# Token attention fused with the first expert dispatch, and a re-split dispatch: one TensorE, ScalarE and VectorE program in place of two

## What is computed

```python
# token attention, per image; xn is the token's row norm (mean 0, variance 1 over 128 channels)
scores = xn @ xn.T
x = x + softmax(scores) @ xn
# mixture of experts: per token
xn = (x - mean(x)) * rsqrt(var(x) + eps)
scores = xn @ Wg + bg                       # 8 experts
topk_vals, topk_idx = top_k(scores, 2)
gates = softmax(topk_vals)
out = sum over the 2 chosen experts: gate * (gelu(xn @ W1[e] + b1[e]) @ W2[e] + b2[e])
```

## Time and profile before

| | us |
|---|---|
| median of 3 runs | 2566.55 (2564.8 to 2569.15) |
| profiled execution | 2577.6 |
| its span in the trace | 2575.5 |

### The profile page before, as it was taken

One profiled execution on the slowest core, in us unless ns is written; L12 is line 12 of the kernel. 1 busy time (PEld: TensorE's weight loads), 2 busy tenths in 40 slices (PEclk: granted clock), 3 DMA queues, 4 the chain that ended last, 5 costly groups with the idle time before them and its releaser, 6 DMA issues. The chain is left out here.

```text
span 2575.5 us, 54220 instructions
## 1 busy us (share of the span) xinstructions
PE 1827.2 (71%) x16654; PEld 1267.9 (49%) x16654; DVE 1792.5 (70%) x5249; ACT 1274.2 (49%) x2662; POOL 1443.4 (56%) x1552
## 2 busy tenths in 40 slices
PE   7999998998943222777745788888432209999993
PEld 4555556775742221555533355555322207777772
DVE  5888886775767662666642899998476627888873
ACT  5777764655620001555530678776210007777760
POOL 4555560000137773777765466666477745676675
PEclk9999998998965555999975899998555559999995
DMA  5000000000022113656637000000441136777757
GB/s 115 3 0 0 0 1 1 0 1 1 0 81 92 54 54 107 176 169 177 182 113 180 1 1 0 0 0 2 115 160 54 54 112 217 231 230 230 232 172 299
DMA packets 191639, 232.97 MB, mean 90 GB/s; under 512 B 60384, under 2 KB 157397, under 8 KB 184046
## 3 DMA queue, kind: packets, MB, share of 16 engines
q1 hardware_dynamic: 164302, 172.32, 23.0%
q0 software_dynamic: 26880, 52.27, 6.0%
q10 hardware_dynamic: 288, 6.42, 0.6%
HBM read 155.37 MB, written 79.23 MB: 91 GB/s over the span
## 5 line engine op out<-in xcount | busy, mean ns | idle before, releaser
L2311 POOL DMA_INDIRECT expert_out<-moe_yr,moe_to x448 | 494.8, 1104 | 268.9 <-DVE moe_yr L2290 148.0
L2082 POOL DMA_INDIRECT expert_rows<-d_row,d_pos x392 | 380.2, 970 | 167.8 <-issue 118.0
L2226 ACT ACTIVATE moe_ah<-moe_hps,moe_w 128x512 f32<-128x512 f32 (+1 forms) x336 | 230.3, 686 | 204.4 <-PE moe_hps L2176 202.2
L2267 DVE TENSOR_TENSOR moe_hl<-moe_ah,moe_hh 128x512 fp32r<-128x512 f32 (+1 forms) x336 | 236.3, 703 | 98.0 <-ACT moe_hh L2231 92.2
L1851 PE MATMUL d_rank<-d_seen,d_below 128*128 128x32 bf16 (+1 forms) x50 | 10.4, 207 | 346.7 <-DVE d_seen L1983 346.7
L1851 PEld LDWEIGHTS d_rank<-d_seen,d_below 128*128 128x128 bf16 x50 | 5.2, 104 | 351.3 <-DVE d_seen L1983 351.3
L549 POOL TENSOR_TENSOR window_pr<-window_pr,window_rc 113x392 f32<-113x392 f32 x128 | 108.9, 851 | 107.1 <-DVE window_rc L493 107.0
L2174 PE MATMUL moe_hps<-moe_xh,moe_w 128*128 128x512 f32 (+1 forms) x336 | 138.5, 412 | 35.1 <-DMA moe_w<-moe_split 25.6
L2162 PE MATMUL moe_xps<-ident,moe_xb 128*128 128x128 f32 x448 | 73.5, 289 | 119.4 <-DMA moe_xb<-expert_rows 119.4
L1939 DVE TENSOR_SCALAR d_row<-d_xt,d_mv,d_rs 128x128 f32<-128x128 f32 x196 | 67.1, 404 | 111.9 <-DMA expert_rows<-d_row,d_pos 111.8
L2186 PE MATMUL moe_yps<-moe_hh,moe_w 128*128 128x512 f32 (+1 forms) x336 | 143.7, 428 | 0.9 <-DVE moe_hl L2267 0.9
(11 more groups left out here) (262 smaller groups left out, 5482.1 us busy)
## 6 DMA issues: line engine op xcount, KB each, us to landing
moe_w<-moe_split SPq DMA_DIRECT2D x56, 1026.5 KB
moe_xb<-expert_rows SPq DMA_DIRECT2D x112, 264.0 KB
moe_w<-moe_split SPq DMA_DIRECT2D x56, 449.5 KB
final_yy<-expert_out SPq DMA_DIRECT2D x28, 448.0 KB
c_yy<-expert_out SPq DMA_DIRECT2D x48, 256.0 KB
expert_out<-moe_yr,moe_to POOLq DMA_INDIRECT x448, 3.4
X<-in_x SPq DMA_DIRECT2D x32, 196.0 KB
expert_rows<-d_row,d_pos POOLq DMA_INDIRECT x392
```

The source lines that it names most:

```text
L2082: pool.indirect_dma_start(out=rows_dram, out_offset=bass.IndirectOffsetOnAxis(ap=pos[j][:, i, k:k + 1], axis=0), in_=row[j][:, i, :], in_o ...
L2226: act.activation(ah[n % NH][0:P, :], hps[n % 3][0:P, :], func, bias=bias(b, k)[0:P]).then_inc(h_done, 1)
L2267: dve.tensor_tensor(hl[n % NH][0:P, :], ah[n % NH][0:P, :], hh[n % NH][0:P, :].bitcast(F32), ALU.subtract).then_inc(hl_done, 1)
L2311: pool.indirect_dma_start(out=y_dram, out_offset=bass.IndirectOffsetOnAxis(ap=to[j][:, t:t + 1], axis=0), in_=yr[j][:, t, :], in_offset=No ...
```

## The change

Two stages become one, and the dispatch is written anew as a class that both places use.

- `token_dispatch_phase` replaces the token stage and "d2". One step of the token pipeline handles a group (392 tokens) and, where enough tokens have their residual, a chunk of the dispatch (512 tokens). `sorting_steps` gives the step at which a chunk is transposed: with residuals done up to group s-2 at step s, chunks fall at steps 3, 4, 5, 7, 8, 9, 11, and so on to 34, three chunks in four steps with one extra. A chunk is transposed in step s, gets logits and is chosen in s+1, and is weighed and placed in s+2.
- PSUM is shared out anew: one bank for the centred tokens (two before), one bank `tps` for both the turned probabilities and the turned tokens, two for transposed tiles, and one bank `small` for logits and ranks together. So `logits(c)` waits for `at_done` of chunk c-1, an instruction of `place`.
- GpSimd does nothing but scatters. The product of the probabilities (L1078 before) is on VectorE (`probs`), and the copy of the turned tokens out of PSUM (L1014 before) is on ScalarE (`v_out`).
- The row norm of the dispatch is on ScalarE as four Identity activations for a chunk with `scale` the reciprocal deviation and `bias` the negated product of mean and reciprocal deviation, which VectorE makes (`negmean`). Two column copies of VectorE also go to ScalarE (`names`); two more instructions of `weigh` and the addition of the region's base in `place` are gone (the base is in the ranks' product, which is why REGION is now a multiple of 1024). The second gate weight has its sign turned, and the expert stage adds where it subtracted.
- SyncE writes the pads once the table is there, without waiting for the scatters.
- "d3" uses the same class, with four banks of transposed tiles, one step for each chunk.

The core of the diff (the bodies of `choose`, `stats`, `table`, `positions` and of the token attention's functions are those of before but for names, buffers and what is said above):

```diff
@@ module level @@
-REGION = TOKENS + BLOCK
+REGION = 13 * 1024
+CHUNKS = chunk_tiles()
...
+class Dispatch:
+    NR = 3
...
+    def pads(self, sp):
+        sp.wait_ge(self.loaded, 16 * 8)
+        spare = self.rows_dram[EXPERTS * REGION:EXPERTS * REGION + BLOCK].rearrange("(t p) c -> p t c", p=C)
+        sp.dma_start(spare, self.pad[:, :, :]).then_inc(self.padded, 16)
+        sp.wait_ge(self.tab, 2)
+        for x in range(EXPERTS):
+            n = sp.value_load(self.offs[0:1, x:x + 1], min_val=0, max_val=EXPERTS * REGION - BLOCK)
+            sp.dma_start(self.rows_dram[bass.ds(n, BLOCK)].rearrange("(t p) c -> p t c", p=C), self.pad[:, :, :]).then_inc(self.padded, 16)
+        for j in range(2):
+            sp.wait_ge(self.w_stored[j], 32 * EXPERTS // 2)
+        sp.wait_ge(self.b_stored, 16)
+        sp.wait_ge(self.padded, 16 * (EXPERTS + 1))
...
+    def logits(self, pe, c):
+        t0, nt = CHUNKS[c]
+        if c >= 1:
+            pe.wait_ge(self.at_done, c)
+        for i in range(nt):
+            last = pe.matmul(self.small[:, i * EXPERTS:(i + 1) * EXPERTS], self.sh.X[:, (t0 + i) * C:(t0 + i + 1) * C], self.wgc[:, :],
+                             start=True, stop=True, skip_group_check=True)
+        last.then_inc(self.log_mm, 1)
...
+    def norm(self, act, q):
+        c, t0, nt, o = QUADS[q]
+        j = c % self.NR
+        act.wait_ge(self.nm_done, q + 1)
+        act.wait_ge(self.rs_done, q + 1)
+        if c >= self.NR:
+            act.wait_ge(self.scattered[j], 16 * self.scatters(c - self.NR))
+        for i in range(nt):
+            last = act.activation(self.row[j][:, o + i, 0:C], self.xt[q % len(self.xt)][:, i * C:(i + 1) * C], ACT.Identity,
+                                  bias=self.nm[q % 2][:, i:i + 1], scale=self.rs[c % 2][:, o + i:o + i + 1])
+        last.then_inc(self.normed, 1)
+    def gate(self, act, c):
+        nt = CHUNKS[c][1]
+        act.wait_ge(self.gap_done, c + 1)
+        if c >= 1:
+            act.wait_ge(self.den_done, c)
+            act.wait_ge(self.col_done, c)
+        act.activation(self.ex[:, 0:nt], self.gap[:, 0:nt], ACT.Exp).then_inc(self.ex_done, 1)
+    def names(self, act, c):
+        t0, nt = CHUNKS[c]
+        j = c % self.NR
+        act.wait_ge(self.loaded, 16 * 8)
+        if c >= self.NR:
+            act.wait_ge(self.scattered[j], 16 * self.scatters(c - self.NR))
+        act.activation(self.row[j][:, 0:nt, C], self.tokens[:, t0:t0 + nt], ACT.Copy).then_inc(self.named, 1)
+        act.wait_ge(self.idf_done, c + 1)
+        act.activation(self.row[j][:, 0:nt, C + 1], self.idf[:, 0:nt, 0], ACT.Copy).then_inc(self.named, 1)
...
+    def prepare(self, dve):
+        dve.memset(self.count[0][:, :], 0.0).then_inc(self.count_done, 1)
+        dve.memset(self.base16[:, :], 0.0).then_inc(self.ready, 1)
+        dve.wait_ge(self.loaded, 16 * 8)
+        dve.wait_ge(self.ready, 1)
+        dve.tensor_copy(self.base16[0:1, :], self.base8[0:1, :]).then_inc(self.ready, 1)
+        dve.tensor_copy(self.below[:, :], self.below_f[:, :]).then_inc(self.ready, 1)
+        dve.tensor_copy(self.ones[:, :], self.ones_f[:, :]).then_inc(self.ready, 1)
+        dve.wait_ge(self.centred, 1)
+        dve.tensor_copy(self.wgc[:, :], self.small[:, 0:EXPERTS]).then_inc(self.ready, 1)
...
+    def negmean(self, dve, q):
+        c, t0, nt, o = QUADS[q]
+        dve.wait_ge(self.rs_done, q + 1)
+        if q >= 2:
+            dve.wait_ge(self.normed, q - 1)
+        dve.scalar_tensor_tensor(out=self.nm[q % 2][:, 0:nt], in0=self.mv[q % 2][:, 0:nt, 0], scalar=-1.0, in1=self.rs[c % 2][:, o:o + nt],
+                                 op0=ALU.mult, op1=ALU.mult).then_inc(self.nm_done, 1)
...
+    def weigh(self, dve, c):
+        nt, j = CHUNKS[c][1], c % self.NR
+        row = self.row[j]
+        dve.wait_ge(self.ex_done, c + 1)
+        if c >= 1:
+            dve.wait_ge(self.g0_done, c)
+        dve.tensor_scalar(self.den[:, 0:nt], self.ex[:, 0:nt], 1.0, None, ALU.add).then_inc(self.den_done, 1)
+        dve.wait_ge(self.den_done, c + 1)
+        if c >= self.NR:
+            dve.wait_ge(self.scattered[j], 16 * self.scatters(c - self.NR))
+        dve.reciprocal(row[:, 0:nt, C + 2], self.den[:, 0:nt]).then_inc(self.g0_done, 1)
+        dve.wait_ge(self.g0_done, c + 1)
+        dve.scalar_tensor_tensor(out=row[:, 0:nt, C + 3], in0=self.ex[:, 0:nt], scalar=-1.0, in1=row[:, 0:nt, C + 2],
+                                 op0=ALU.add, op1=ALU.mult).then_inc(self.col_done, 1)
+    def place(self, dve, c):
+        nt, j, h = CHUNKS[c][1], c % self.NR, c % 2
+        dve.wait_ge(self.pos_mm, c + 1)
+        if c >= 1:
+            dve.wait_ge(self.spot_done, c)
+        dve.tensor_tensor(self.at[:, 0:nt, :, :], self.pick[h][:, 0:nt, :, :],
+                          self.ranks(nt).rearrange("p (t e) -> p t e", e=EXPERTS)[:, :, None, :].to_broadcast([C, nt, 2, EXPERTS]),
+                          ALU.mult).then_inc(self.at_done, 1)
+        dve.wait_ge(self.at_done, c + 1)
+        if c >= 1:
+            dve.wait_ge(self.pos_done, c)
+        dve.tensor_reduce(self.spot[:, 0:nt, :], self.at[:, 0:nt, :, :], AX_X, ALU.add).then_inc(self.spot_done, 1)
+        dve.wait_ge(self.spot_done, c + 1)
+        dve.tensor_copy(self.pos[j][:, 0:nt, :], self.spot[:, 0:nt, :]).then_inc(self.pos_done, 1)
...
+    def scatter(self, pool, c):
+        nt, j = CHUNKS[c][1], c % self.NR
+        pool.wait_ge(self.pos_done, c + 1)
+        pool.wait_ge(self.normed, LAST_QUAD[c] + 1)
+        pool.wait_ge(self.col_done, c + 1)
+        pool.wait_ge(self.named, 2 * c + 2)
+        for i in range(nt):
+            for k in range(2):
+                pool.indirect_dma_start(out=self.rows_dram, out_offset=bass.IndirectOffsetOnAxis(ap=self.pos[j][:, i, k:k + 1], axis=0),
+                                        in_=self.row[j][:, i, :], in_offset=None).then_inc(self.scattered[j], 16)
...
+def sorting_steps(groups_done):
+    turns, step = [], 0
+    for c, t0, nt, o in QUADS:
+        while groups_done(step) * T < (t0 + nt) * C:
+            step += 1
+        turns.append(step)
+        step += 1
+    return turns
+def token_dispatch_phase(nc, sh, kind, e, wsplit, rows_dram):
...
+    LEAD = 4
...
+        cps, st, tps, sps, ops_ = ps("cen", [C, 512]), ps("st", [C, 512]), ps("turn", [C, 512]), ps("sps", [C, 512]), ps("ops", [C, 512])
+        d = Dispatch(nc, sh, sb, sem, kind, e, wsplit, rows_dram, [ps(f"xt{i}", [C, 512]) for i in range(2)], ps("small", [C, 512]))
...
+            for s in range(-LEAD, last_step):
+                if group(s + 1):
+                    scores(s + 1)
+                if group(s + 3):
+                    var(s + 3)
+                if group(s - 1):
+                    values(s - 1)
+                if group(s):
+                    turn(s)
+                if group(s + 2):
+                    tokens(s + 2)
+                for c in chunks(s - 2):
+                    d.positions(pe, c)
+                for c in chunks(s - 1):
+                    d.logits(pe, c)
+                for q in quads(s):
+                    c, t0, nt, o = QUADS[q]
+                    pe.wait_ge(res_done, -(-(t0 + nt) * C // T))
+                    d.turn(pe, q)
+                if group(s + 4):
+                    mean(s + 4)
+            d.totals(pe)
...
+            for s in range(-LEAD, last_step):
+                if group(s + 1):
+                    shift(s + 1)
+                if group(s - 1):
+                    residual(s - 1)
+                for q in quads(s - 1):
+                    d.negmean(dve, q)
+                if group(s + 1):
+                    probs(s + 1)
+                if group(s + 3):
+                    norm(s + 3)
+                for c in chunks(s - 2):
+                    d.weigh(dve, c)
+                    d.place(dve, c)
+                for c in chunks(s - 1):
+                    d.choose(dve, c)
+                for q in quads(s):
+                    d.stats(dve, q)
+                if 1 <= s <= EXPERTS:
+                    d.split_low(dve, s - 1)
+            dve.wait_ge(res_done, NG)
+            d.table(dve)
...
+            for s in range(-LEAD, last_step):
+                if group(s + 1):
+                    expo(s + 1)
+                for q in quads(s - 1):
+                    d.rstd(act, q)
+                if group(s + 3):
+                    rstd(s + 3)
+                if group(s):
+                    turned(s)
+                if group(s + 2):
+                    v_out(s + 2)
+                for q in quads(s - 1):
+                    d.norm(act, q)
+                for c in chunks(s - 2):
+                    d.gate(act, c)
+                    d.names(act, c)
+                if 1 <= s <= EXPERTS:
+                    d.split_high(act, s - 1)
+                if group(s + 4):
+                    square(s + 4)
...
@@ dispatch_phase, the expert stage and build @@
+        turns = sorting_steps(lambda step: NG)
...
```

(37 more changed lines are left out.)

## The result

The changed kernel takes 2521.9 us in the median of four runs (2519.8 to 2524.2), the kernel before beside it 2567.9 (2564.8 to 2572.7): ratio 0.982, 95% interval 0.980 to 0.984. The forecast was 2515, in a range of 2470 to 2560: the sign, the size and the mechanism came out. Within the sum the end of each dispatch was about 7 us short, and in the fused stage the term for the clock, about 9 us too large, covered that.

A forecast was written before the change was run, and what follows sets the result against it. VectorE's queue, through waits on ScalarE and TensorE, was taken to bound the fused stage, GpSimd's scatters the second dispatch. Fused stage -47, clock +12, second dispatch -16.5 make -51.5: 2515 us on the median's scale, range 2470 to 2560.

The forecast's parts named there:

- the term for the clock: Fused stage: TensorE's low clock adds 1.4 us a step, 41 us in 29 steps, of which 30% was taken, +12.
- VectorE's queue bounds the fused stage: Fused stage: VectorE's queue, through waits on ScalarE and TensorE, takes 13.3 us a chunk against GpSimd's 10.1.
- The forecast's layout of a full step: Fused stage, step with place, choice and stats, timed from VectorE's shift: `gate` ends at 6.25, the step takes 12.3 us.
- The row norm on ScalarE: Fused stage: four 128-column activations ahead of `gate`, between 0.8 and 2.4 us, taken as 1.1.
- its sum at the high clock: Attention and first dispatch fused, steps laid out at the high clock: 380 us against 427, -47.
- The pads: End of second dispatch: 13.0 us from first pad to next stage become a barrier's 1.7, -11.3.
- the earlier start: Second dispatch: the first chunk is placed sooner, ahead of the second split of the weights, about -5 us.
- Low clock throughout: Rival: TensorE stays at the low clock in the fused stage, total 2546 us; chance 0.20.
- GpSimd as the bound: Rival: GpSimd's scatters remain the bound, fused stage 315 us, total 2438; chance 0.09.
- Slower by a mean step of 12.2 us: Rival: single banks at the low clock delay the residual, 12.6 us a step, total 2579, deciding from 12.2; chance 0.09.
- the sign that the prediction named for this rival: Fused stage: VectorE waits for the residual's product in most steps, 2.1 us late in every step.
- Second dispatch unchanged: Rival: the pads or the earlier start are not saved in the second dispatch, total 2531 us; chance 0.05.

The follow-up runs named there:

- gate_early: Against the changed kernel: ScalarE's exponential for the gate moved right behind the sorting's deviation, ahead of the attention's deviation, turned tiles and row norm; 2482.1 us.
- norm_dve: Against the changed kernel: the row norm back on VectorE behind the attention's norm, without `negmean`, in both dispatches; 2510.4 us.
- pe_order: On gate_early: logits in the scores' bank, `names` ahead of turned tiles, and TensorE's queue in the order VectorE needs results; 2455.8 us, 0.956 of the kernel before.
- busy: Against the changed kernel: TensorE makes the centred tokens of each group from the eighth on three times instead of once; 2543.5 us.
- fill: Against the changed kernel: TensorE makes two products that nobody reads where it stands for the old positions before the logits; 2510.5 us.

## Why the prediction was right, point by point

**VectorE's queue bounds the fused stage: right.** The forecast's layout of a full step against the rows, from the shift on: norm ends 3.45, measured 3.19; `gate` 6.25, measured 6.58; `at` begins at 6.9, measured 7.11; logits read 8.1, measured 9.29; step 12.3, measured 13.18. The product on VectorE took 0.37 (0.36 taken). gate_early then showed the wait to be on the path, as the step's layout had it. Chunks were placed 13.6 us apart (826.67 to 867.60 for three), 13.3 in the layout. The first scatter was foreseen for 648 and came at 648.65; chunk 20 was placed at 915.9 against 914; the last scatter ended at 961.7 against 960.

**The row norm on ScalarE was mis-sized:** 1.50 us for four against 1.1, which I had taken from the 98-column row. The two bounds, 0.8 and 2.4, held. The Trainium skill's page "ScalarE: Activation LUTs", section "Rules for kernel authors", gives the estimate of 1.6 named in the prediction, and it was nearer to the 1.50 than the nearest row was. Its advice to have multiplications on VectorE agrees with norm_dve, 15 us shorter, but the gain there came from the place in ScalarE's queue: the four take 1.37 us on VectorE and 1.50 on ScalarE.

**The clock term was too large for the sum, and why is only in part shown.** The clock was low half the time (0.75), not the 30% assumed; by the prediction's 1.4 us a step that would be +20, where it took +12. Without the end, the fused stage took 2.7 us more than its sum at the high clock. All of that lies ahead of the first chunk, whose step began 42.8 us into the stage (40 in the prediction); from there to the placing of chunk 20 it took 290 us, as in the sum. That does not mean that the low clock cost nothing. The logits took 1.88 us at 0.50 in the full step, where 0.95 was laid out, and VectorE stood 2.30 us for the residual's product in the step at 843.49, where the layout had no wait. Against that the layout was too long elsewhere: choice and statistics take 3.89 us after the logits are read, not 4.15, and the kind of step that has a choice but no `place` 8.67, not 9.4. So part of the agreement is luck, and what the low clock costs in the whole stage is not measured. The Trainium skill's page "TensorE: Matmul & The Clock Gate", section "HAM oscillation — how this bites in real kernels", was right about the pattern (the granted clock went back and forth between 0.50 and 1.00), but the 41 us that I put on it did not follow.

**The pads: the step that failed.** "13.0 us from first pad to next stage become the 1.7 of a barrier" took the pads as the only thing at the end of the stage. GpSimd's drain ran under them and takes almost as long: the pads' removal gave 5 us a stage, and the end of the fused stage cost 10.9, not 4.1. In the second dispatch -16.5 became -9.9: the earlier start gave 6.7 (first scatter 16.6 us into the stage, 23.3 before) where 5 was taken, and the end 4.6 where 11.3 was taken; the scatters themselves took 1.3 more. In the fused stage the missing 6.8 us were covered by the clock term, which was 9.3 too large: two errors that cancel, no merit of the sum.

**The rivals.** Low clock throughout: no, the granted clock was 0.69 in the mean of the stage. GpSimd as the bound: not in this order of the queues, and yes in pe_order. Slower by a mean step of 12.2 us: no, it was 10.2. But the sign that the prediction named for this rival did show: VectorE waited for the residual's product in 17 steps between 640 and 900, that is in most, 20.3 us in all. That is 1.2 us a time, where the rival had 2.1 in every step, and pe_order, with the values ahead in TensorE's queue, brought it to 2.5 us between 640 and 880. Second dispatch unchanged: no, though two fifths of its gain failed to come.

## What to carry to other kernels

When two stages are fused into one hand-ordered pipeline, lay out one step engine by engine and look for the small instruction that others wait for behind a long one: moving a 0.2 us exponential ahead of 4 us of work that VectorE was not waiting for was worth 41 us here, nearly as much as the whole change, and ordering TensorE's queue by who waits took another 20 off the stage. Before you count a hidden operation's removal as a gain, look for what runs under it, in the queue instructions too: a drain on another engine can be nearly as long. And when a moved operation is late, look up in which step its result is used before you price the lateness.

## What the runs showed of the hardware that I had not expected

- GpSimd's drain at the end of a stage with software-made scatters is not free: 7570 ns behind 196 scatters, the same to the nanosecond in all twelve first dispatches with that number (7578 in the kernel before), 7652 with one empty scatter more and 8713 with 14 more (82 ns for each), 3323 ns with 28 more, and 702 ns behind the 224 of the expert stages. A bound on the row number changes nothing. It stands only among the queue instructions, not on the timeline.
- TensorE's clock moved between its two levels again and again within one stage. In the piece from 690 to 731.6 work that nobody reads raised the mean from 0.75 to 0.79 (busy, fill), and an order of the queues that lets the engines wait less raised it to 0.96 (pe_order). There it was 0.90 to 0.96 from 650 to 816 and fell to 0.54 from 816 to 857.
- An activation of 128 columns took 0.38 us in a row of four (1.50), where four of 98 columns over 49 partitions took 0.77 together. The two differ in more than their size (the first have a scale and a bias for each partition), so what makes the difference is not shown.
